# Splitting the shared network's weights and first rows, and its first block of products, inside the convolution's tail

## The reference

```python
shared_sum = _ffn(flat_x, shared_w1, shared_w2)            # 4096 rows, 512 -> 2*256 -> 512
gate_logits = flat_x @ gate_w + expert_bias                # 7 per row
aff = sigmoid(gate_logits); topk_idx = top_k(aff, 2)       # two experts a row
score = where(mask, aff, -1.0).T
_, sel_idx = top_k(score, capacity)                        # 585 rows an expert
out = vmap(_ffn)(flat_x[sel_idx], routed_w1, routed_w2)
routed_sum = zeros.at[sel_idx].add(out * w)
return shared_sum + routed_sum      # _ffn: h = x @ w1; (x1 * silu(x2)) @ w2; flat_x is layer-normed
```

## Time and profile before

| what | before |
|---|---|
| median of 3 runs | 2099.63 us (2096.68 to 2100.72) |
| the profiled execution | 2089.57 us |
| its span, first to last instruction | 2087.3 us, mean granted TensorE clock 0.962 |
| busy: PE, DVE, ACT, POOL | 1906.0, 1394.3, 802.6, 645.0 us (91%, 67%, 38%, 31% of the span) |
| barrier behind the convolution | passed at 1727 us |

### The profile page before, as it was taken

One profiled execution on the slowest core, in us unless ns is written; L12 is line 12 of the kernel. 1 busy time (PEld: TensorE's weight loads), 2 busy tenths in 40 slices (PEclk: granted clock), 3 DMA queues, 4 the chain that ended last, 5 costly groups with the idle time before them and its releaser, 6 DMA issues. The chain is left out here.

```text
span 2087.3 us, 35150 instructions
## 1 busy us (share of the span) xinstructions
PE 1906.0 (91%) x13798; PEld 1618.3 (78%) x13798; DVE 1394.3 (67%) x2817; ACT 802.6 (38%) x1484; POOL 645.0 (31%) x507
## 2 busy tenths in 40 slices
PE   4699999999999989999999998799988998989997
PEld 2477788778787778899999997577777787767886
DVE  5787777777777765655555554478876866784654
ACT  4544545445544442322222221344444443223332
POOL 1333333334333331000000000576665630002563
PEclk7599999999999999999999999899999987999999
DMA  3221122121111105122222221734444434334674
GB/s 118 76 72 62 71 68 76 62 72 62 62 62 62 62 31 192 61 102 101 90 94 101 102 84 48 257 119 145 135 131 131 136 137 139 116 106 157 161 186 64
DMA packets 111750, 214.64 MB, mean 103 GB/s; under 512 B 14242, under 2 KB 34786, under 8 KB 110562
## 3 DMA queue, kind: packets, MB, share of 16 engines
q1 hardware_dynamic: 104194, 195.30, 27.5%
q0 software_dynamic: 7392, 17.11, 4.0%
HBM read 136.11 MB, written 76.34 MB: 102 GB/s over the span
## 5 line engine op out<-in xcount | busy, mean ns | idle before, releaser
L1370 PE MATMUL psum<-kv,toep 128*128 128x288 f32 x1280 | 324.1, 415 | 43.4 <-ACT yx L1418 25.9
L1370 PEld LDWEIGHTS psum<-kv,toep 128*128 128x128 f32 x1280 | 246.6, 194 | 118.4 <-ACT yx L1418 32.0
L168 PE MATMUL psum<-xn_t_h,w_gate_h 128*128 128x256 f32 x768 | 232.7, 303 | 0.9 <-DVE th L292 0.9
L168 PE MATMUL psum<-xn_t_h,w_up_h 128*128 128x256 f32 x768 | 217.5, 283 | 0.0
L169 PE MATMUL psum<-xn_t_l,w_up_h 128*128 128x256 f32 x768 | 217.5, 283 | 0.0
L170 PE MATMUL psum<-xn_t_h,w_gate_l 128*128 128x256 f32 x768 | 217.5, 283 | 0.0
L169 PE MATMUL psum<-xn_t_l,w_gate_h 128*128 128x256 f32 x768 | 217.4, 283 | 0.0
L170 PE MATMUL psum<-xn_t_h,w_up_l 128*128 128x256 f32 x768 | 216.7, 282 | 0.0
L161 POOL TENSOR_TENSOR rstd<-rstd,minus_half 128x2 f32<-128x2 f32 x48 | 34.9, 727 | 562.0 <-DVE rstd L157 562.0
L275 ACT ACTIVATE th<-psum 128x256 f32<-128x256 f32 x192 | 73.6, 383 | 313.1 <-PE psum L170 313.0
L1036 POOL TENSOR_SCALAR_AFFINE_SELECT operands<-operands 128x512 f32<-128x512 f32 x128 | 99.6, 778 | 275.1 <-ACT operands L779 275.1
(11 more groups left out here) (305 smaller groups left out, 4683.6 us busy)
## 6 DMA issues: line engine op xcount, KB each, us to landing
toep<-ssm_padded_scratch SPq DMA_DIRECT2D x64, 256.0 KB, 3.5
kx<-in_ctx_pairs SPq DMA_DIRECT2D x32, 384.0 KB, 4.3
x_scratch<-x_all SPq DMA_DIRECT2D x21, 512.0 KB, 2.8
x_all<-in_x SPq DMA_DIRECT2D x16, 512.0 KB, 3.8
operands<-in_ctx_t SPq DMA_DIRECT2D x16, 512.0 KB, 4.7
xn_t_scratch<-xn_t_h SPq DMA_DIRECT2D x16, 512.0 KB, 2.7
xn_t_scratch<-xn_t_l SPq DMA_DIRECT2D x16, 512.0 KB, 3.8
xn_t_h<-xn_t_scratch SPq DMA_DIRECT2D x16, 512.0 KB, 3.7
```

What stands on the lines that cost most here:

```text
L168: pe.run.matmul(out, lhs[0], rhs[0], start=first, stop=False)
L1370: ins = pe.run.matmul(out, w[:, (o - k) * P:(o - k + 1) * P], pairs, start=(k == 0), stop=(k == o))
```

## The change

The shared weights are loaded during the convolution (behind unit 47), with 1 MB and 0.5 MB into tiles laid over `q_half0`, whose use is over by then. In the tail ScalarE and VectorE split the four pieces of w1 and the four tiles of block 0, and the last turn is block 0's whole hidden product, in place of `logits` 4 and 5. ScalarE normalises blocks 6 and 7 ahead of its copies of `turn` 4 and 5. Behind the barrier `SEEN` is 16: the logits of tiles 16 to 23 (turned before) come first, and the turns and logits of tiles 24 to 31 stand between the parts of block 1, two tiles a part. `affinity` 1 and two ranks (instead of one) follow in parts 3 and 4, `mask` in part 5, `score_turn` in part 6. From then on each block takes nine links instead of eight; the ninth stands inside `out`, behind the second tile. The three small steps that make `first_slot` move from the stage's start into `final`.

```diff
+        w1_raw = early("w1_raw", [P, KT, 2 * FF], starts1[0])
+        w2_raw = early("w2_raw", [P, FT, D], starts1[1])
+        w1_first = [early(f"w1_0_{c}", [P, KT, 2 * FF], at_, F32R) for c, at_ in zip("hl", starts1[2:])]
+        xt_first = [early(f"xt0_{c}", [P, KT, SPAD], at_, F32R) for c, at_ in zip("hl", starts2)]
...
+        def load_expert(n, a, c):
+            sp.wait_ge(expert_low, n * PIECES)
+            sp.run.dma_start(w1_raw[:, :, :], a.rearrange("(k p) n -> p k n", p=P)).then_inc(expert_loaded, 16)
+            sp.run.dma_start(w2_raw[:, :, :], c.rearrange("(k p) n -> p k n", p=P)).then_inc(expert_loaded, 16)
...
             turns += [("turn", 2), ("turn", 3), ("logits", 2), ("tiles", 6), ("tiles", 7), ("logits", 3), ("turn", 4), ("turn", 5),
-                      ("logits", 4), ("logits", 5)]
+                      ("hidden", 0)]
...
+                    elif kind == "hidden":
+                        assert set_of[turn] == 0 and 2 * FT == KT
+                        pe.wait_ge(expert_low, KT)
+                        pe.wait_ge(split_low, BLK)
+                        for f in range(FT):
+                            for half_ in (1, 0):
+                                cols = slice(half_ * FF + f * P, half_ * FF + (f + 1) * P)
+                                for k in range(KT):
+                                    ins = product(bank_t[2 * f + half_][:, 0:NB], [w[:, k, cols] for w in w1_first],
+                                                  [x[:, k, 0:NB] for x in xt_first], k == 0, k == KT - 1)
+                                ins.then_inc(banks.filled[2 * f + half_], 1)
...
                     elif kind == "turn":
+                        if n >= HT - 2:
+                            normalise(n + 2)
                         act.wait_ge(rows_in_banks, n + 1)
...
-                for r in range(HT, TILES):
-                    normalise(r)
+                        if n == HT - 3:
+                            act.wait_ge(expert_loaded, 32)
+                            for k in range(KT):
+                                act.run.copy(w1_first[0][:, k, :], w1_raw[:, k, :]).then_inc(expert_high, 1)
+                            act.wait_ge(summed, N)
+                            for j in range(BLK):
+                                act.run.copy(xt_first[0][:, :, j * P:(j + 1) * P],
+                                             rows[:, j, :].rearrange("p (k n) -> p k n", k=KT)).then_inc(split_high, 1)
...
+                        if n == HT - 4:
+                            dve.wait_ge(expert_loaded, 32)
+                            for k in range(KT):
+                                dve.wait_ge(expert_high, k + 1)
+                                dve.run.tensor_tensor(w1_first[1][:, k, :], w1_raw[:, k, :], w1_first[0][:, k, :].bitcast(F32),
+                                                      ALU.subtract).then_inc(expert_low, 1)
                     elif kind == "tiles":
                         add_residual(n)
                         if n >= HT:
                             statistics(n)
+                        if n == HT:
+                            for j in range(BLK):
...
+                                dve.run.tensor_tensor(xt_first[1][:, :, cols], rows[:, j, :].rearrange("p (k n) -> p k n", k=KT),
+                                                      xt_first[0][:, :, cols].bitcast(F32), ALU.subtract).then_inc(split_low, 1)
...
+                    if n == 3 * N // 4:
+                        sp.wait_ge(turned, TILES // 2)
+                        load_expert(0, io["shared_w1"], io["shared_w2"])
...
-            SEEN = (NBLK - 2) * BLK
+            SEEN, TURNED = (NBLK - 4) * BLK, (NBLK - 2) * BLK
...
-            links = [([("affinity", 1), ("rank", SEEN // 8)], []), ([("mask",)], [])]
-            links += [([], [])] * 6 + [([], [("score_turn",)])]
+            links = [([], [])] * 4 + [([("affinity", 1), ("rank", SEEN // 8)], []), ([("rank", SEEN // 8 + 1)], []), ([("mask",)], []),
+                                      ([], [("score_turn",)])]
...
+            order = [("turn", TURNED + i) for i in range(2)] + [("affinity", 0)] + [("split", j) for j in range(BLK)]
+            order += [("weights", 0, i) for i in range(KT, PIECES)]
+            order += [("logits", i) for i in range(SEEN, TURNED)]
+            def routing(part):
+                for i in range(TURNED + 2 * part, TURNED + 2 * part + 2):
+                    if i + 2 < TOKT:
+                        yield ("turn", i + 2)
+                    yield ("logits", i)
+                if part < SEEN // 8:
+                    yield ("rank", part)
...
-                    before_part, after_part = next(links, ([], []))
+                    before_part, after_part = next(links, ([], [])) if blk else ([], [])
                     order += before_part
+                    if blk == 1 and part < BLK:
+                        order += routing(part)
...
                             order += later[j:j + 1]
+                            if j == 1:
+                                before_part, after_part = next(links, ([], []))
+                                order += before_part + after_part
...
-                    elif name == "hidden":
+                    elif name == "hidden" and at[0]:
```

More of the change, by code:

```diff
@@ L1282, in sbc @@
                 return sbuf(cc, name, shape, dt)
-            q_half = [sbc(f"q_half{i}", [P, KT, HB * S]) for i in range(2)]
+            q_half = [sbc("q_half0", [P, KT, HB * S])]
+            terms = [sbc(f"terms{i}", [P, KB, HR, HR]) for i in range(2)]
+            yx = [sbc(f"yx{i}", [P, KB, 11 * 4]) for i in range(2)]
+            q_half.append(sbc("q_half1", [P, KT, HB * S]))
             toep = [sbc(f"toep{i}", [P, L]) for i in range(3)]
@@ L1751, in build_program @@
             links = iter(links)
-            order = [("turn", SEEN + i) for i in range(BLK)] + [("affinity", 0)]
-            for j in range(2 * BLK):
-                i = SEEN + j
-                if i + BLK < TOKT:
-                    order.append(("turn", i + BLK))
-                order.append(("logits", i))
-                if j < PIECES:
-                    order.append(("weights", 0, j))
-                order.append(("split", j))
-            order += [("rank", c) for c in range(SEEN // 8)]
+            order = [("turn", TURNED + i) for i in range(2)] + [("affinity", 0)] + [("split", j) for j in range(BLK)]
[8 more added lines that the diff above has]
+                    yield ("rank", part)
             for blk in range(NBLK):
-                later = []
+                later = [] if blk else [("split", BLK + j) for j in range(BLK)]
+                order += later
                 if 0 < blk < NBLK - 1:
@@ L1858, in tensor_late @@
                         j = i - SEEN
-                        bank, filled, emptied, n = banks.at("turn", i)
-                        pe.wait_ge(emptied, n + 1)
+                        if i >= TURNED:
+                            bank, filled, emptied, n = banks.at("turn", i)
+                            pe.wait_ge(emptied, n + 1)
                         bank, filled, emptied, n = banks.at(name)
@@ L1990, in scalar_late @@
                         act.run.activation(a, a, ACT.Exp, scale=-1.0).then_inc(affinity_exp, 1)
-                    elif name == "split":
+                    elif name == "split" and at[0] >= BLK:
                         i = at[0]
                         blk, j = i // BLK, i % BLK
-                        if i >= SEEN:
+                        if i >= TURNED:
                             bank, filled, emptied, n = banks.at("turn", i)
@@ L2119, in vector_late @@
                         decide(len(BITS) - 1)
+                        quotient = refused
+                        dve.settle(dve.run.tensor_scalar(quotient[:, :], room[:, 0:1].bitcast(I32), CN.bit_length() - 1, None,
+                                                         ALU.arith_shift_right))
+                        dve.settle(dve.run.tensor_copy(first_slot[:, :], quotient[:, :]))
+                        dve.run.tensor_scalar(first_slot[:, :], first_slot[:, :], float(NT * P), float(P - 1), ALU.mult, ALU.add)
                         dve.run.tensor_scalar(over[:, :], score_t[:, :], cand[:, 0:1].bitcast(F32), 0.0, ALU.is_gt, ALU.add,
@@ L2294, in sync_late @@
                         sp.wait_ge(split_low, (blk + 1) * BLK)
-                        bank, filled, emptied, n = banks.at("logits")
-                        sp.wait_ge(filled, n + 1)
+                        if blk >= SEEN // BLK:
+                            bank, filled, emptied, n = banks.at("logits")
+                            sp.wait_ge(filled, n + 1)
                         sp.wait_ge(x3_loaded[blk % 2], 16 * (blk // 2))
```

51 lines of the change are left out of this document (24 added, 27 removed).

## The result

| what | before | after |
|---|---|---|
| median | 2099.53 us of 9 (2096.53 to 2103.57) | 2105.52 us of 9 (2104.44 to 2109.01) |
| after to before | | 1.0035, 95% interval 1.0025 to 1.0044 |
| profiled execution, its span | 2089.57, 2087.3 us | 2104.70, 2103.0 us |

The kernel is slower by 0.35%, by that ratio 7.3 us (5.2 to 9.2); the two medians are 6.0 us apart. That is inside the range of the prediction and on the side to which it leaned, but about twice its sum of +3.6 us.

A forecast was written before the change was run, and what follows sets the result against it. PE, which the other engines wait for, was taken to bound the changed stretch, with gaps. Terms -2.3 (through block 1), +3.9 and +2.0 sum to +3.6 us, added to the 2099.6 us median: 2103.2 us, range 2094 to 2111.

The forecast's parts named there:

- Step 1: Convolution's tail up to the barrier: PE ends last after the 48 products, barrier passed at 1729.3 instead of 1727.1, 2.2 us later.
- The load's price of 0: Shared weight load during the convolution: taken to cost 0, at most 1.8 us; rival that it holds up units, +5.4, chance 0.05.
- Step 2: From the barrier to the last logits, partly at the lower clock: last logits done at 1763.9, ends 1757 and 1779.
- clock stays low: Rival: logits between the parts keep PE's granted clock at 0.50 through block 1, +11 us; chance 0.13.
- high clock behind the barrier: Rival: the clock stays high there, last logits at 1757, net -5.1 us; chance 0.20.
- Step 3: VectorE's chain from last logits to score, 11.1 us: PE stands 5.5 us, block 1 ends at 1778.4 against 1780.7, -2.3 us.
- The table loads: Two added ScalarE loads of 1.28 us from alternating Exp and Silu: costed at nothing; 2.7 us more if in the chain.
- Step 4: Ninth link inside the outs of blocks 2, 3 and 4: PE stands 1.3 us in each, +3.9 us.
- Step 5: Blocks 5 and 6, waits for final total, choose, slots and tables: 9.5 us against 7.4 before, +2.0 us, ends 0 and +4.
- Behind block 6: Late stretch of the kernel: equal length from block 7 on, only shifted; gathers' later ids cost nothing.

The follow-up runs named there:

- the second profile: Kernels before and after the change each run and profiled once more, no edit: 2100.93 us before, 2107.03 us after.
- the early link: Changed kernel with the ninth link's VectorE step moved ahead of each block's first split: ratio to before 1.0007, and 1.0015 when measured again.
- few logits: Changed kernel with the products of tiles 16 to 23 behind the barrier cut from four to one: 2091.93 us.
- the kernels with eight links: Changed kernel without the ninth link inside the outputs, eight links a block as before: 2109.95 us, ratio 1.0074.
- with the logits in the tail: Changed kernel with logits 4 and 5 put back in the tail, ahead of block 0's hidden product: 2111.31 us, ratio 1.0073.

## Why the prediction was right, and where its sum was off

- **Step 1, the barrier: +2.2 forecast, +0.5 and +2.0 measured.** It is passed at 39.9, before at 39.4. The clock was at its upper level for all 48 products, as I had assumed; the two last turns began at 22.2 (1713.01 less 1690.82), not at 23.9. The four row differences did cost their 2.4 us (2.49 in DVE's row), but the residual of tiles 6 ahead of them began at 11.7 from the zero, not at 13.3, since in this execution the turns of tiles 6 and 7 ran at the upper clock (32 in 3.69 us; the earlier trace rows has 23 in 4.6). In the second profile they did not, and the barrier was passed at 41.4, against my 41.6; before passed it at 39.4 again. So the step was right and only the clock in front of it varies. The load's price of 0 stands within what can be seen.
- **Step 2, the last logits: forecast 76.2 from the zero, they end at 78.6.** Subtracting the barrier's error, this stretch took 4.1 us more, and again 4.1 in the second profile. The lower clock held for 24 us, from 44.5 to 68.4 (1735.3 to 1759.2), where I expected 16, from 46 to 62, and let one part bring it back. It is the beginning of the rival "clock stays low", ended by the second part and the first outputs behind it. The other rival, high clock behind the barrier, is excluded: 20 us of busy PE at 0.50. So where the Trainium skill (TensorE: Matmul & The Clock Gate, The two states you'll see) ties the lower state to an idle engine, this stretch disagrees, as the earlier trace rows did.
- **Step 3, the score's wait: 5.5 forecast, 5.28 measured.** From the affinity to the score's transposes took 10.9 us, 11.1 forecast. The table loads are in no wait: the load of 1.28 us ran at 1766.08, and the exponential only at 1769.75, as soon as VectorE's sum was there. The sum of steps 1 to 3 was -2.3; by the outputs of block 1 it is -0.6 in one profile and +1.9 in the other, against 96.4 and 96.5. This term was short by 1.7 to 4.2 us, nearly all of it in the clock of step 2.
- **Step 4, the ninth link: +3.9 forecast.** The three waits are 1.12, 1.08 and 1.09 us in place of 1.3, and each block is 1.35 us longer than one without the link (18.4 us): 4.1. Taken away by the early link, it gave 3.7. Right by mechanism and size.
- **Step 5, blocks 5 and 6: +2.0 forecast, +2.9 in waits.** The waits were forecast at 9.5 us and are 10.3, against 7.4 before. On top of them, behind the final total's wait of 1.94 us nine wide matmuls start 0.43 us apart instead of 0.23, 1.7 us; in the second profile that fall came behind the first table's wait of 2.95 us instead. I had seen such a fall behind the score's wait and priced it there only. But the second profile of before has one too, behind `place`, so it is a price that either kernel may pay and no clear part of the change. From the outputs of block 3 to those of block 6 after takes 6.8 us more in the first pair and 4.3 in the second; less the third link's 1.35 that is 5.5 and 2.9.
- **Behind block 6: nothing forecast, nothing found.** From there to block 7's outputs it takes 21.1 and 24.8 us before, 24.3 and 22.6 after.

So -0.6 to +1.9, +4.1 and +2.9: 6 to 9 us, and 9.0 by the starts at block 6 in both pairs, against 6.0 by the medians and 7.3 by the ratio. The mechanisms were right. The term that was mis-sized is step 2: the lower clock was priced per stage as the earlier trace rows showed it, with one part to end it, and among the clumps of small work in the new order it held 8 us longer, which at half the rate is the 4.1 us. The waits of step 5 add 0.9. A part of the closeness is luck: in the first profile the barrier came 1.7 us sooner against before than forecast, and hid as much of step 2's error.

As for the purpose of the change, block 0's outputs do come 10.3 us sooner. But 4.5 of that are the waits of 1.15 and 3.33 us that before has ahead of these outputs and after has not yet had. Block 1 is 9.7 us longer in the first pair: 5.3 of score wait, and 4.4 of turns and logits (the last two clumps) that used to come ahead.

## What to carry to other kernels

When work is moved ahead of a barrier, ask what the chain that starts behind it was using that time for. Here the routing's chain on VectorE began 16 us later (total 0 at 92.4 in place of 76.4), and its steps had to be packed more densely into the blocks that remain; here each of three places where two of them meet the in-order matmul stream cost 1.1 us, and behind some of the longer stops the clock fell as well. The cheap cure lay in order, not in volume: a step put ahead of a split instead of behind it gave 4 to 6 us, a rank put into an idle stretch 3 to 4 us more, and an activation queued ahead of copies that wait took a further 2.7 us out of the profile, which the ratios (0.9994, then 0.999) can't tell.

## What the runs showed of the hardware

**The clock.** Between the zero and 100 us behind it TensorE spent 37.5 us at its lower level in both profiles of before, 37.5 in the first of after and 47.8 in the second (summed from the granted clock of 1 us windows). The second of after has 7 us of it in the turns of tiles 6 and 7 ahead of the barrier, where the first has none. Common to both is one piece of 24 us behind the barrier, from the logits of tiles 16 to 23 over the first two parts of block 1 to the first matmuls of block 0's outputs. The clock came back 3.6 to 4.8 us behind the last small work ahead of a long run of wide matmuls in two traces (1754.4 to 1759.2 in after; 1745.9 to 1749.5 with few logits).

**A product held while gathers are issued.** In 6 of 12 profiles (all but those of the kernels with eight links and with the logits in the tail), of before and of changed kernels alike, the last product of block 7 starts 1.9 to 2.8 us later than its matmuls would allow, and begins within 0.2 us of the start or the end of the last of GpSimd's 15 gather issues. DVE and POOL in after:
```profile
1915.36 0.69 DVE L2107 TENSOR_TENSOR pr<-sg,psum 128x512 f32<-128x512 f32 x1 [6.17 <-remote]
...
1914.36 0.97 POOL L2327 DMA_INDIRECT rows<-rows_scratch,ids  x1 [0.30 <-issue]
```
It starts 0.03 us behind the end of the last issue; in the second profile of before it starts at 1909.00, between two issues (the last began at 1909.11). In the undisturbed profiles the same wait is 3.42 us long and other gathers are still to come. The difference, 1.9 to 2.8 us, is passed on to the slot transposes (4.80 us of wait in after, 2.01 where the product is on time), and is a part of why two runs of one kernel differ (in before, 3.7 of the 11.6 us between its two spans lie between the outputs of blocks 6 and 7). The Trainium skill (SBUF — State Buffer, Who interferes with whom) says that a VectorE instruction with two SBUF inputs contends with a GpSimd one that reads SBUF. This product has one SBUF and one PSUM input, so that rule as stated doesn't cover it, and no run here tells what does.
